# A decoder layer on one core of Trainium2: queries and keys of self attention in tiles of 128 tokens instead of 112

## What is computed

```python
x = x * rsqrt(mean(square(x), -1) + eps) * w        # RMS norm over the 512 features
q, k, v = split(x @ Wq), split(x @ Wk), split(x @ Wv)   # 16 heads of 64
q = q / maximum(norm(q), 1e-12) * (q_gamma + 1) * 8     # norm of each head's 64 values
k = k / maximum(norm(k), 1e-12) * (k_gamma + 1) * 8
sim  = tanh(einsum('bhid,bhjd->bhij', q, k) / 50) * 50 * 64**-0.5
out  = einsum('bhij,bhjd->bhid', softmax(sim), v)
x    = layernorm(x + out @ Wo)
```

## Time and profile before

| | before |
|---|---|
| runs | 1807.08, 1807.59, 1809.39 us, median 1807.59 |
| profiled execution | 1808.88 us, its span 1806.4 us |
| PE busy in the span | 1752.7 us (97%) |
| DVE busy | 1412.5 us (78%) |
| ACT busy | 1172.5 us (65%) |
| POOL busy | 1113.4 us (62%) |
| mean granted clock of TensorE | 0.992 of full speed |

### The profile page before, as it was taken

The page is one execution under the profiler, slowest core; times in us unless marked ns, Lnnn a source line. Parts: engine busy times, 40 slices in busy tenths (PEclk is TensorE's granted clock), DMA queues, the critical chain, the costliest instruction groups (busy, mean ns, idle before and its releaser), DMA issues.

```text
span 1806.4 us, 37455 instructions
## 1 busy us (share of the span) xinstructions
PE 1752.7 (97%) x13942; PEld 1475.7 (82%) x13957; DVE 1412.5 (78%) x3240; ACT 1172.5 (65%) x2680; POOL 1113.4 (62%) x1250
## 2 busy tenths in 40 slices
PE   8999999999998899999999999999999999988997
PEld 7777777778877899999999999899899999974443
DVE  6777778787887677777777788777776777787888
ACT  6878887756755566666666667666666656654664
POOL 3434445664566586786686655677777788551554
PEclk9999999999998999999999999999999999999999
DMA  5223323111105423432432523314313341543553
GB/s 206 76 67 94 103 75 111 46 32 46 48 22 173 137 90 98 152 100 77 153 103 74 167 97 86 112 49 125 96 61 101 96 114 52 125 106 92 129 129 97
DMA packets 141106, 176.80 MB, mean 98 GB/s; under 512 B 63884, under 2 KB 99088, under 8 KB 140928
## 3 DMA queue, kind: packets, MB, share of 16 engines
q1 hardware_dynamic: 122392, 138.15, 25.3%
q0 software_dynamic: 14656, 28.92, 5.9%
q10 hardware_dynamic: 3880, 7.35, 1.3%
HBM read 109.25 MB, written 50.46 MB: 88 GB/s over the span
## 4 chain that ended last, share of the span: by engine, by line
PE 74%; DVE 10%; ACT 5%; POOL 5%; DMA 3%; issue 3%; ACTq 0%; POOLq 0%; DVEq 0%
PE att_ps_T L552 7%; PE att_ps_SA L1755 5%; PE att_ps_P L1731 5%; PE att_ps_SB L612 4%; PE att_ps_P L1719 4%; PE att_ps_P L552 4%; PE att_ps_P L1783 4%; PE att_ps_SB L600 3%; PE att_ps_O L1719 3%; PE att_ps_T L1719 3%; PE att_ps_P L1769 3%; PE att_ps_T L1731 3%; PE att_ps_O L1731 2%; PE att_ps_P L1794 2%; POOL sa_p_lo L423 2%
## 5 line engine op out<-in xcount | busy, mean ns | idle before, releaser
L1537 POOL TENSOR_TENSOR ca_pr<-ca_pr,ca_rec 112x750 f32<-112x750 f32 x256 | 366.6, 1453 | 187.2 <-DVE ca_rec L2017 184.3
L423 POOL TENSOR_TENSOR sa_p_lo<-sa_pr,sa_p_hi 112x448 fp32r<-112x448 f32 x128 | 146.8, 1162 | 210.5 <-ACT sa_p_hi L718 209.7
L1902 ACT ACTIVATE ca_big<-att_ps_P 126x384 fp32r<-126x384 f32 (+1 forms) x254 | 105.3, 449 | 66.1 <-PE att_ps_P L1769 64.9
L1896 ACT ACTIVATE ca_pr<-att_ps_SA,ca_nmax 112x750 f32<-112x750 f32 x128 | 113.7, 888 | 22.0 <-DVE ca_nmax L2013 11.2
L887 DVE RECIPROCAL sa_sums<-sa_sums 128x224 f32<-128x224 f32 x64 | 99.1, 1548 | 33.8 <-ACT sa_sums L727 33.6
L2022 DVE TENSOR_TENSOR ca_big<-att_ps_P,ca_big 126x384 fp32r<-126x384 f32 (+1 forms) x254 | 119.8, 498 | 6.2 <-ACT ca_big L1902 5.9
L2013 DVE TENSOR_REDUCE ca_nmax<-att_ps_SA 112x1 f32<-112x752 f32 x128 | 119.1, 931 | 1.3 <-PE att_ps_SA L1755 1.2
L2013 DVE TENSOR_REDUCE ca_nmax<-att_ps_SB 112x1 f32<-112x752 f32 x128 | 119.1, 930 | 0.0
L1731 PE MATMUL att_ps_P<-ca_w_hi,ca_ct 128*126 128x256 f32 x558 | 114.2, 284 | 1.4 <-DVE ca_q_lo L1996 1.4
L1896 ACT ACTIVATE ca_pr<-att_ps_SB,ca_nmax 112x750 f32<-112x750 f32 x128 | 113.3, 885 | 0.1
L1769 PEld LDWEIGHTS att_ps_P<-att_ident,ca_pr 64*126 64x126 f32 (+1 forms) x1524 | 85.5, 138 | 15.2 <-issue 10.8
(11 more groups left out here) (354 smaller groups left out, 6618.9 us busy)
## 6 DMA issues: line engine op xcount, KB each, us to landing
ct_kept<-ca_ct SPq DMA_DIRECT2D x8, 1134.0 KB, 9.3
ca_ct<-ct_kept POOLq DMA_DIRECT2D x8, 1134.0 KB, 7.7
ct_kept<-ca_ct SPq DMA_DIRECT2D x8, 1116.0 KB, 12.3
ca_ct<-ct_kept POOLq DMA_DIRECT2D x8, 1116.0 KB, 10.0
sa_xin<-in_x_dram SPq DMA_DIRECT2D x16, 448.0 KB, 3.7
xt_kept<-ca_xt SPq DMA_DIRECT2D x8, 896.0 KB, 5.2
ca_xt<-xt_kept POOLq DMA_DIRECT2D x8, 896.0 KB, 5.3
ternary<-ca_stage SPq DMA_DIRECT2D x36, 172.0 KB, 1.9
```

Of the source, the lines that this page charges most:

```text
L423: pool.tensor_tensor(p_lo[:, h % NB, :], pr[:, h % NB, :], f32(p_hi[:, h % NB, :]), ALU.subtract).then_inc(p_split, 1)
L1537: pool.tensor_tensor(w, w, rec[:, h % PB, c:c + 1].to_broadcast([R, S]), ALU.mult).then_inc(norm_done, 1)
L1896: act.activation(pr[:, h % PB, c, :].rearrange("r (a s) -> r a s", a=2), two_halves(psum[slot]), ACT.Exp, bias=nmax[:, h % PB, c:c + 1], a ...
```

## The change

Queries and keys are projected in tiles of 128 tokens that go on over the borders of the batches. Four batches have 896 tokens, which are 7 tiles, so of each four batches the first three project two new tiles and the last one only one (`TILES_OF`). In passes 3, 7, 11 and 15 the units Q1 and K1 hence do nothing: each engine only raises the semaphore. Values stay in blocks of 112 rows. With it come:

- x is needed earlier, since the second tile of a batch reaches into the next one: AHEAD becomes 3, xt_hi and xt_lo become rings of 2 x 224 + 64 columns, Q1 waits for x of the next pass, q_hi, q_lo, k_hi and k_lo become rings of two batches, and a T unit of the second of four batches is evacuated in two pieces for q and two for k (`RING_PIECES`).
- The guard of a row is needed on the row of its tile. So SP spreads the sums of squares by small transfers (`spread_squares`), ahead of the next batch's rows, and DVE makes the guard in a step of its own (U), behind HK1.
- The buffer of the squares (sq) and that of the tanh (th) have two places instead of four, and p_lo shares its place with pr.
- In steps where the next pass has one tile, PE's order is `WITH_ONE_TILE`, in which V0 and V1 stand earlier.

The core of the diff:

```diff
-    AHEAD = 2
+    AHEAD = 3
+    PERIOD = 4
+    XW = 2 * N + HALF
+    TILES_IN = PERIOD * N // P
+    TILE_COLUMNS = [[0, P], [2 * P, 3 * P], [HALF, HALF + P], [2 * P + HALF]]
+    TILES_OF = [[0, 1], [2, 3], [4, 5], [6]]
+    TILES_READY = [[0], [1, 2], [3, 4], [5, 6]]
+    RING_PIECES = [[(0, 0, 2 * P)], [(0, 2 * P, P + HALF), (P + HALF, 0, HALF)], [(0, HALF, 2 * P)], [(0, 2 * P + HALF, P)]]
...
-    sq = in_early("sq", [R, 4, DM])
-    xt_hi = in_early("xt_hi", [P, KC, N], F32R)
+    sq = in_early("sq", [P, 2, DM])
+    xt_hi = in_early("xt_hi", [P, KC, XW], F32R)
...
-    th = in_late("th", [R, NB, 2 * N])
     pr = in_late("pr", [R, NB, 2 * N])
+    in_late.at = at["late"]
+    p_lo = in_late("p_lo", [R, NB, 2 * N], F32R)
...
+    th = in_late("th", [R, 2, 2 * N])
...
-    UNITS = """XT0 XT1 Q0 K0 Q1 K1 V0 T0 V1 T1 T2 T3""".split()
-    units = [(u, f"P{i % 3}") for i, u in enumerate(UNITS)]
+    UNITS = """Q0 K0 Q1 K1 V0 T0 V1 T1 T2 T3 XT0 XT1""".split()
+    units = [(u, f"P{(i + 2) % 3}") for i, u in enumerate(UNITS)]
...
     def load_rows(src, before):
         if before:
+            sp.wait_ge(ss_done, before(2, 2))
+            if number(before) < B:
+                spread_squares(number(before))
             sp.wait_ge(filled[slot["XT1"]], filled_count("XT1", before))
-            sp.wait_ge(ss_done, before(2, 2))
...
     def project(u, at, arriving=False):
         i, c = "QKV".index(u[0]), int(u[1])
+        if u[0] != "V" and c >= len(tiles(at)):
+            pe.sem_inc(filled[slot[u]], 1)
+            return
...
+        if u == "Q1":
+            for t in range(2):
+                pe.wait_ge(drained[slot[f"XT{t}"]], drained_count(f"XT{t}", lambda per, k: at(per, k) + per))
         pe.wait_ge(drained[slot[u]], free_count(u, at))
+        if u[0] == "V":
+            rows, col = R, ring_at(at) + c * R
+        else:
+            rows, col = P, TILE_COLUMNS[number(at) % PERIOD][c]
...
-            for c in range(2):
-                mm = pe.transpose(ps(u)[:, i * N + c * R:i * N + c * R + R], t[:, c, p * P:p * P + P], ident[0:R, 0:R])
+            for c in range(len(tiles(at))):
+                col = (2 * i + c) * P
+                mm = pe.transpose(ps(u)[:, col:col + P], t[:, c, p * P:p * P + P], ident[:, :])
...
+    WITH_ONE_TILE = steps("""S1 O0 O1 S2 Q0+ O2 O3 K0+ S3 O4 O5 Q1+ V0+ O6 O7 K1+ V1+ Y0 T0+ T1+ S0+ T2+ Y1 T3+ X+++""")
...
-        for name, n in ORDERS[g]:
+        short = batches[1] and len(tiles(batches[1][1])) == 1
+        for name, n in WITH_ONE_TILE if short else ORDERS[g]:
...
     def head_squares(u, at):
         act.wait_ge(filled[slot[u]], filled_count(u, at))
-        act.activation(sq[:, 2 * c + i, :], ps(u)[0:R, :], ACT.Square).then_inc(sq_done, 1)
+        if c >= len(tiles(at)):
+            act.sem_inc(sq_done, 1)
+            return
+        if c:
+            act.wait_ge(reduced[0], at(2, i + 1))
+        elif number(at):
+            act.wait_ge(reduced[1], at(2, i - 1))
+        act.activation(sq[:, i, :], ps(u)[:, :], ACT.Square).then_inc(sq_done, 1)
...
+            for start, to, width in RING_PIECES[number(at) % PERIOD]:
+                q = act.activation(q_hi[:, p, to:to + width], ps(u)[:, start:start + width], ACT.Copy)
...
     def mean_squares(at):
-        dve.tensor_scalar(guard[:, :], ss[:, :], 1e-24 / DM, 1e-24 * RMS_EPS, ALU.mult, ALU.add).then_inc(rows_done, 1)
...
+    def guards(at):
...
+        dve.wait_ge(ss_spread, spread_count(m))
+        dve.tensor_scalar(guard[:, of], tile_ss[:, of], 1e-24 / DM, 1e-24 * RMS_EPS, ALU.mult, ALU.add).then_inc(guard_done, 1)
...
                     if isinstance(b, int) and g * B + b + n == 0:
-                        if name == "HQ0":
-                            weights_lo(0)
-                            weights_lo(1)
-                            gammas()
-                        elif name == "G":
+                        if name == "G":
                             small_weights()
+                    if isinstance(b, int) and g * B + b + n == 1 and name == "XT0":
+                        weights_lo(0)
+                        weights_lo(1)
+                        gammas()
```

More of the change, by code:

```diff
@@ L311, in step_before, with pieces_of, spread_count, spread_squares @@
         return at(plan.uses[slot[u]], 1)
+    def pieces_of(m):
+        pieces = []
+        for c in range(2):
+            token, end = m * N + c * R, m * N + c * R + R
+            while token < end:
+                n = min(end, token // P * P + P) - token
+                pieces.append((c, token - m * N - c * R, n, token // P, token % P))
+                token += n
+        return pieces
+    def spread_count(m):
+        return 16 * sum(len(pieces_of(n)) for n in range(m + 1))
     def sync(sp):
+        def spread_squares(m):
+            for c, r, n, t, row in pieces_of(m):
+                sp.dma_start(tile_ss[row:row + n, t:t + 1], ss[r:r + n, m % 2, c:c + 1]).then_inc(ss_spread, 16)
         def load_weights(g, which):
@@ L574, in scores @@
             heads = [f"S{2 * p + odd}" for odd in range(2)]
+            ring = ring_at(at)
             for u in heads:
@@ L784, in do @@
             if name == "X":
-                row_squares(at, not isinstance(b, int) or g * B + b + AHEAD > 0)
+                row_squares(at)
             elif name[0] == "W":
@@ L2682, in layers @@
         late = fixed.at + EARLY
-        mem = {"held": base, "early": fixed.at, "late": late, "rows": late + 79968, "rows_end": late + 79968 + 6144, "small": late + 95968, "ca_live": fixed.at + 34400, "ca_scored": fixed.at + 34400 + 7168,
+        mem = {"held": base, "early": fixed.at, "late": late, "rows": late + 79968, "rows_end": late + 79968 + 6144, "small": late + 96384, "ca_live": fixed.at + 34400, "ca_scored": fixed.at + 34400 + 7168,
                "end": nc.sbuf_base}
```

175 lines of the change are left out of this document (114 added, 61 removed).

## The result

The changed kernel takes 1858.72 us (median of 4 runs, 1857.35 to 1860.53), the kernel before beside it 1808.49 us. The ratio is 1.0274, with a 95% interval of 1.0258 to 1.0291: 50 us slower, where 30 were forecast and 1856 was the upper end of the range. The profiled execution has a span of 1856.4 us, 50.0 more than before.

A forecast was written before the change was run, and what follows sets the result against it. PE's own work was taken to bound self attention. From 1808.9 us, 9.3 (one-tile waits), 8.6 (clock), 6.9 (start), 2.6, 3 and 0.5 (two-tile steps) were added and 1.3 subtracted, giving 1838; range 1820 to 1856.

The forecast's parts named there:

- waits less saved work, four one-tile steps: Steps 2, 6, 10 and 14: waits exceed the 22.3 us of PE work saved, 9.3 us longer in all.
- clock in them: One-tile steps: PE's clock falls five times behind the waits, costing 8.6 us.
- start: Before step 0: Q0 starts 5.2 us later, at 16.5, plus one clock fall of 1.7: 6.9 us.
- two-tile steps (transposes, pieces, guard): Other self attention steps: wider transposes +2.6 us, extra and wider pieces +3, moved guard +0.5.
- hand-over and cross attention: From self attention's end onward: no added time forecast, 0 us.
- the step that decides: One-tile steps: V0 waits for K0's bank P0 until DVE has scaled K0, 3.7 us in half 0, 5.9 in half 1.
- T1: Half 1's one-tile steps: T1 waits for V0's bank, evacuated behind T0; T0 at 446.5 us, T1 at 449.0.
- S0: One-tile steps, half 0: S0 waits for T0's evacuation, put at 1.7 us and no longer covered by V1.
- Rival (a): One-tile steps: the banks do not bind and the whole 22.3 us come back, giving 1798 us; chance 0.07.
- V1: One-tile steps: PE waits 2.6 to 3 us ahead of V1 for the release of K1's bank by DVE.
- the sentence that has step 14 absorb 1.3 us of the wait of the earlier trace: End of self attention: step 14's delay absorbs about 1.3 of PE's 1.39 us wait for cross attention's rows, leaving +3.2.
- The wider weight loads: PE's projections: loads of 128 columns stay hidden under matmuls and cost nothing; 9 us if on the path.

The follow-up runs named there:

- e8: Changed kernel with 14 (half 0) and 23 (half 1) idle matmuls filling PE's wait ahead of V0 in the four one-tile steps: 1848.48 us, ratio 1.0214.
- e3: Changed kernel with V0 of one-tile passes in bank P1 instead of P0, in half 1 also evacuated ahead of T0: 1825.09 us, ratio 1.0096.
- e4: Changed kernel; in the step ahead of step 0, ACT squares the rows of the batch three ahead at the step's end: 1855.16 us, ratio 1.0251.
- e5: Changed kernel; at the start, idle matmuls run while PE awaits batch 1's rows, and ACT squares batch 2's rows between Q1's and K1's squares: 1851.36 us, ratio 1.0243.
- e11: Changed kernel with only POOL's layer norm scaling M moved in half 1 from the step's end to behind B0: 1851.16 us, ratio 1.0230.
- e10: e9 with the value weights for half 1 split later by POOL and DVE at the border of the halves: 1806.07 us, ratio 0.9979.
- e1: Changed kernel with PE's old order also in the four one-tile steps, so V0 stands behind O6 and O7 again: 1827.75 us, ratio 1.0113.
- e9: e3 plus adapted PE, ACT and DVE lists in one-tile steps, e5's start, and POOL's M behind B0 in half 1: 1807.62 us, ratio 0.9990.

## Why the prediction was right, and where it was wrong

Each term beside what it measured. The growths are those of the table; for the split of the first two, e8's. The forecast cut the steps at their ends, the table cuts them at S0, so a column gives the same forecast cut there: S0 was to come at 137.6 in step 2 and at 449.3 in step 11, which is 1.7 and 5.0 us behind the marks of before. That is 13.4 us for four steps. What was to be won back behind S0 (0.3 us twice and 0.5 twice by narrow T2 and T3, the 1.2 us of the earlier trace rows, the 1.3 us of the earlier trace rows) falls to the rows of the two-tile steps and of the hand-over.

| term | forecast, us | forecast at the marks, us | measured, us |
|---|---|---|---|
| waits less saved work, four one-tile steps | 9.3 | 13.4 | 10.2 |
| clock in them | 8.6 | 8.6 | 9.5 |
| start | 6.9 | 6.9 | 14.5 |
| two-tile steps (transposes, pieces, guard) | 6.1 | 3.8 | 8.3 |
| hand-over and cross attention | 0 | -1.8 | 7.4 |
| sum | 30.9 | 30.9 | 49.9 |

**Right: the step that decides.** V0 waits for K0's bank, 3.58 and 5.78 us against 3.7 and 5.9, and e3 takes it away by another bank (in half 0 by the bank alone). The waits of T1 (2.1 us) and S0 (1.1 to 1.9) came as said. Rival (a) was excluded by the earlier trace rows, and rightly.

**Right in kind, too long: V1.** It was to wait 2.6 to 3 us for the release of K1's bank and waited 1.4 to 1.8. From V0's start to V1's the forecast had 7.3 us in half 0 and 6.9 in half 1; e8, where the clock does not blur it, has 5.7 and 5.8 to 6.1, some 5 us less over the four steps. I had DVE finish the reciprocal of I3, 1.55 us, before the empty step behind it releases the bank. DVE's timeline of the changed kernel:

```profile
146.23 1.55 DVE L1004 RECIPROCAL sa_sums<-sa_sums 128x224 f32<-128x224 f32 x1 [5.32 <-ACT sa_sums L819]
```

V1 starts at 146.83, in the middle of it: here the step that only raises a semaphore did not wait for the arithmetic ahead of it on its engine.

**Right in the sum, by luck: the clock.** I priced a fall at 1.7 us and took five. There were four, one in each one-tile step, and the clock was low for 7 to 10 us each time, 3.4 to 5.1 us of work; but a part of that lies under the wait itself, where nothing runs. What is left is 2.4, 2.6, 1.9 and 2.6 us (after less e8). So fewer falls than forecast, each dearer, made up the same sum.

**Wrong: the start.** Q0 was forecast for 16.5 and came at 17.41. The step of the prediction that failed is its sum for the start, which ends with Q0's start and one fall of the clock and puts nothing for what lies between Q0 and the first scores. I followed x of batch 1 on PE and left out the same move on ACT: the squares of batch 2's rows, which the deeper prefetch brings into this step, stand in ACT's list ahead of Q0's squares, and those rows had not landed. Against the kernel before, Q0 starts 6.1 us later, K1 9.0, T0 12.2 and S0 12.3. The 2.9 us up to K1 are this wait, and e4 takes them away. The 3.2 up to T0 are the fall of the clock behind it (1.7) and T0's own wait for DVE's scaled q, 2.24 us instead of 0.68, which stays in e4 and e5 and whose cause no run separates. Then comes, in this execution, another fall in step 0 (2.2). e5 gets back 6.5 of the 15.1.

**Wrong: the hand-over.** The step that failed is the sentence that has step 14 absorb 1.3 us of the wait of the earlier trace rows. But the rows of cross attention are not tied to PE; they are behind a store that waits for POOL's M, at the end of POOL's step. In the changed kernel M starts only when DVE's last reciprocal has come and POOL has split the outputs of the last pair; POOL and SP:

```profile
583.09 2.04 POOL L479 TENSOR_TENSOR sa_y<-sa_y,sa_rs 112x512 f32<-112x512 f32 x2
...
585.16 0.30 SPq L427 DMA_DIRECT2D x<-sa_y  x1
...
587.61 0.93 SPq L1526 DMA_DIRECT2D ca_xin<-x  x1
```

The store cannot go before M has ended at 585.13, 3.4 us ahead of S0 of pass 15 (4.6 in the kernel before), and context and rows follow it in one go, where before the context had been issued 2 to 4 us ahead of the rows. Measured from S0, PE asks for the rows only 0.4 us earlier than before, and they are issued 0.7 us earlier; but they come 9.4 us behind their issue instead of 7.5, and PE waits 2.9 us instead of 1.4. That the loads issued together slow each other down is the likely reason, and is not isolated. e11 shows some 8 us for the early store (7.6 by the medians), more than the wait; what is beyond the wait are falls of the clock and later waits, which no run separates, and the 7.4 us of the table are one execution's.

**Too low: the two-tile steps**, 8.3 for 6.1, or for 3.8 at the marks. Two places make most of the difference, and the forecast has neither. The step to pass 8, at the border of the halves, grew by 2.67, where POOL's splits of new weights come late (e10). The step to pass 12 grew by 1.32 and in e1, e3, e9 and e10 by -0.2: that is the fall of the clock behind T1's wait in the one-tile step ahead of it (444 to 448 us). The wider weight loads cost some 1 us, and not nothing: in the changed kernel a matmul with 128 columns comes every 234 ns, one with 112, as V still has, every 232 as before, and there are 672. The load of 128 columns (groups by form, mean ns) is still under it:

```profile
L626 PEld LDWEIGHTS att_ps_P<-sa_w_hi,sa_xt_hi 128*128 128x128 f32 x108 | 20.4, 189 | 3.7
```

With the 175 ns of the earlier trace rows that is 14 ns for 16 columns. By the Trainium skill ("TensorE: Matmul & The Clock Gate", LDWEIGHTS) it would be 13 ns, so the slope agrees; its level, 107 ns for 128 columns, is lower than the row's 189.

The range ended at 1856 because the terms' bounds were counted for the parts that I had priced. At the marks, the start (7.6 us too low), the hand-over (9.2) and the two-tile steps (4.5) miss 21 us, and the waits, 3.2 too high, hide a part of it; what is left are the 19 us that are missing.

**Where the expected gain went.** 22.3 us of PE's work did fall away. The empty places were not free: Q1 covered the softmax of heads 6 and 7 (e1) and the evacuation of K0 (the change as made), and, as I read the waits without a run for it alone, Q1 and K1 covered the last pair's outputs ahead of the hand-over. With the bank changed, the lists adapted, and start, hand-over and border mended, the one-tile steps end 16.3 us earlier than before, of the 22.3 that were there to gain, and the kernel is 0.2% faster than before (e10).
